# Edge convolution on one core: one-hot row picks in float32r instead of bf16, and a second picked tile in two chunks of five

## What is computed

```python
h = relu(layernorm(x))                                   # no scale, no shift
feat = concat([h[dst], h[src] - h[dst]], axis=-1)
m = relu(feat @ W1 + b1) @ W2 + b2                       # one row per edge
out = x + where(isneginf(segment_max(m, dst)), 0, segment_max(m, dst))
```

## Time and profile before

| what | value |
|---|---|
| median of 3 runs | 3946.11 us (3945.49 to 3949.43) |
| profiled execution, first to last instruction (span) | 3943.7 us |
| what lies around the span (median less span; no separate time of the profiled execution is recorded) | 2.4 us |
| setup, until the first chunk is turned | 488.7 us |
| 313 chunks, until the last store of states | 3798.5 us |
| last part (carry between lanes, gather of maxima, output) | 145.2 us |

### The profile page before, as it was taken

One profiled execution on the slowest core, in us unless ns is written; L12 is line 12 of the kernel. 1 busy time (PEld: TensorE's weight loads), 2 busy tenths in 40 slices (PEclk: granted clock), 3 DMA queues, 4 the chain that ended last, 5 costly groups with the idle time before them and its releaser, 6 DMA issues.

```text
span 3943.7 us, 67318 instructions
## 1 busy us (share of the span) xinstructions
PE 3133.0 (79%) x16627; PEld 1717.1 (44%) x16627; DVE 2582.5 (65%) x7825; ACT 955.1 (24%) x3840; POOL 2963.9 (75%) x3103
## 2 busy tenths in 40 slices
PE   3100099999999999999988889898898898888820
PEld 2000055555555555555544444444444454444410
DVE  5210088788777777787777777777677777767731
ACT  4420022222222222222222222222222222222200
POOL 6777777777777777777777777777777777777766
PEclk8555599999999999999999999999999999999965
DMA  9994133333333333333333333333333333333332
GB/s 372 376 415 192 36 93 95 95 95 94 95 92 91 94 95 95 93 94 91 91 88 85 88 89 87 85 88 87 85 88 88 85 88 88 85 87 87 84 91 49
DMA packets 226373, 443.25 MB, mean 112 GB/s; under 512 B 76740, under 2 KB 81721, under 8 KB 215363
## 3 DMA queue, kind: packets, MB, share of 16 engines
q1 hardware_dynamic: 77508, 220.45, 17.0%
q0 software_dynamic: 100496, 106.38, 13.0%
q10 hardware_dynamic: 47977, 112.13, 7.6%
HBM read 220.98 MB, written 217.71 MB: 111 GB/s over the span
## 4 chain that ended last, share of the span: by engine, by line
POOL 42%; issue 19%; SPq 19%; DMA 9%; PE 9%; DVE 1%; ACT 0%; POOLq 0%; ACTq 0%; DVEq 0%
POOL rows L440 38%; SPq L375 10%; DMA a_edges<-rows 8%; PE ps_g L739 8%; SPq L373 5%; POOL a_rows L496 2%; POOL a_edges L463 2%; SPq L374 2%; PE ps_m L758 1%; SPq L390 1%; DMA row_idx<-in_src_dram 1%; PE ps_t L749 1%; DVE state L983 0%; DVE a_fill L952 0%; DMA a_fill<-a_edges 0%
## 5 line engine op out<-in xcount | busy, mean ns | idle before, releaser
L440 POOL DMA_INDIRECT rows<-b_table,src_idx x2780 | 2657.2, 956 | 847.7 <-issue 844.6
L739 PE MATMUL ps_g<-shared,dst_all 128*128 128x512 bf16 x11433 | 2578.1, 380 | 1.6 <-DVE dst_all L1012 1.4
L739 PEld LDWEIGHTS ps_g<-shared,dst_all 128*128 128x128 bf16 x11433 | 1106.1, 98 | 1222.5 <-issue 12.3
L952 DVE SCALAR_TENSOR_TENSOR a_fill<-a_fill,keep 128x64 f32<-128x64 f32 x3125 | 874.1, 280 | 352.3 <-DMA a_fill<-a_edges 329.4
L983 DVE SCALAR_TENSOR_TENSOR state<-state,keep,ps_m 128x64 f32<-128x64 f32 x3125 | 861.2, 276 | 110.3 <-PE ps_m L758 64.6
L600 ACT ACTIVATE dst_all<-ident_h,key_octet 128x128 f16<-128x128 f16 x309 | 123.6, 400 | 2233.3 <-DVE state L983 2232.6
L969 DVE TENSOR_TENSOR rows<-rows,a_fill 128x512 f32<-128x512 f32 x625 | 279.5, 488 | 521.2 <-DMA rows<-b_table,src_idx 520.9
L758 PE MATMUL ps_m<-w_diag,zt 128*128 128x128 f32 x3126 | 426.7, 284 | 225.0 <-ACT zt L622 220.7
L610 ACT ACTIVATE dst_all<-ps_g,dst_all 128x64 f32<-128x64 f32 x2472 | 539.2, 343 | 0.0
L758 PEld LDWEIGHTS ps_m<-w_diag,zt 128*128 128x128 f32 x3126 | 384.3, 193 | 342.8 <-ACT zt L622 326.3
L749 PE MATMUL ps_t<-ident,rows 128*128 128x128 f32 x1563 | 224.0, 274 | 224.9 <-DVE rows L969 224.9
(11 more groups left out here) (122 smaller groups left out, 441.3 us busy)
## 6 DMA issues: line engine op xcount, KB each, us to landing
a_edges<-rows SPq DMA_DIRECT2D x80, 1250.0 KB, 14.9
a_fill<-a_edges SPq DMA_DIRECT2D x312, 320.0 KB
states<-state ACTq DMA_DIRECT2D x312, 320.0 KB
rows<-b_table SPq DMA_DIRECT2D x4608, 0.2 KB
rows<-b_table,src_idx POOLq DMA_INDIRECT x2780, 2.5
a_fill<-b_table ACTq DMA_DIRECT2D x12, 256.0 KB, 8.8
shared<-in_x_dram SPq DMA_DIRECT2D x5, 560.0 KB
b_table<-shared ACTq DMA_DIRECT2D x5, 560.0 KB
```

The lines of the kernel that those rows point to most:

```text
L440: nc.gpsimd.indirect_dma_start(out=rows[:, c % RING, t * C:(t + 1) * C], out_offset=None, in_=b_table, in_offset=at(src_idx[:, q % SRC_RIN ...
L739: last = nc.tensor.matmul(ps_g[:, half, :], key_is[:, half, g, :], table[:, g, t, :], start=(g, t) == (0, 0), stop=g == PAGES - 1)
L952: nc.vector.scalar_tensor_tensor(here, before, flag(c, 0, t), here, ALU.mult, ALU.add).then_inc(fill_step, 1)
```

## The change

The table holds two parts per value in place of three: the float with its lower 12 mantissa bits cleared, and the rest. Both are stored as float32r, and the one-hot matrices too, so a pick is 12 x 2 + 1 = 25 matmuls. The chunks c from 3 on with c % 5 in (1, 3) have two picked tiles, and POOL gathers one tile less there. Three key matrices (`KEY_RING`) are held in place of two, and two of `masked`; `ps_g` keeps two banks. Key matrices and `masked` move to the memory of `blocks` and `dst_all`. The last tiles of a chunk are the picked ones, and SP's tile is the one ahead of them.

```diff
-    PARTS = 3
+    PARTS = 2
+    TOP_BITS = -(1 << 12)
+    PICKS_MOST = 2
     def picks_in(c):
-        return FIRST_PICK <= c < CHUNKS
+        if not FIRST_PICK <= c < CHUNKS:
+            return 0
+        return 2 if c % 5 in (1, 3) else 1
+    def picks_of(c):
+        return [(picks_below(c) + i, i) for i in range(picks_in(c))]
+    KEY_RING = 3
...
-        return CHUNK - 1 - helped(c) if picks_in(c) else CHUNK
+        return CHUNK - picks_in(c) - helped(c)
...
+        table = nc.alloc_sbuf_tensor_at("table", [P, PAGES, PARTS, OCTET * C], F32R, offset=shared_at)
...
+        key_is = [nc.alloc_sbuf_tensor_at(f"key_is{s}", [P, PAGES, P], F32R, offset=at_byte)
+                  for s, at_byte in enumerate((blocks_at, blocks_at + PAGES * P * 4, dst_all_at))]
...
             def mask(c):
-                n = pick_number(c)
-                act.wait_ge(picked, n + 1 + FREE)
-                act.wait_ge(octets_marked, c // BATCHED + 1)
-                act.wait_ge(chosen, n + FREE)
-                for o in range(OCTET):
...
+                for n, i in picks_of(c):
+                    act.wait_ge(picked, n + 1 + FREE)
+                    act.wait_ge(octets_marked, c // BATCHED + 1)
+                    act.wait_ge(chosen, n - 1 + FREE)
+                    for o in range(OCTET):
...
-                for t in range(PARTS):
-                    if t >= 1:
-                        act.wait_ge(page_left, 1 + g * (PARTS - 1) + t)
-                    nc.scalar.activation(table[:, g, t, :], page[:, g % 2, :], ACT.Copy).then_inc(page_part, 1)
+                act.wait_ge(page_cut, g + 1)
+                nc.scalar.activation(table[:, g, 0, :], page_top[:, :].bitcast(F32), ACT.Copy).then_inc(page_part, 1)
...
-            def pick(c, pages):
-                n = pick_number(c)
+            def pick(n, pages):
                 half = n % 2
                 if pages[0] == 0:
                     pe.wait_ge(keys_matched, n + 1 + FREE)
                     pe.wait_ge(octet_masked, n - 1 + FREE)
                 for g in pages:
                     for t in range(PARTS if g < PAGES - 1 else 1):
-                        last = nc.tensor.matmul(ps_g[:, half, :], key_is[:, half, g, :], table[:, g, t, :],
+                        last = nc.tensor.matmul(ps_g[:, half, :], key_is[n % KEY_RING][:, g, :], table[:, g, t, :],
...
-                if picks_in(c + PICK_AHEAD):
-                    pick(c + PICK_AHEAD, range(PAGES_FIRST))
+                for n, i in picks_of(c + PICK_AHEAD)[:1]:
+                    pick(n, range(PAGES_FIRST))
                 for g, n in groups(tiles):
...
-                if picks_in(c + KEYS_AHEAD):
-                    turn_keys(c + KEYS_AHEAD)
-                if picks_in(c + PICK_AHEAD):
-                    pick(c + PICK_AHEAD, range(PAGES_FIRST, PAGES))
+                turn_keys(c + KEYS_AHEAD)
+                for n, i in picks_of(c + PICK_AHEAD):
+                    pick(n, range(PAGES_FIRST if i == 0 else 0, PAGES))
...
+                nc.vector.tensor_scalar(page_top[:, :], page[:, g % 2, :].bitcast(I32), TOP_BITS, None,
+                                        ALU.bitwise_and).then_inc(page_cut, 1)
+                dve.wait_ge(page_cut, g + 1)
+                nc.vector.tensor_tensor(table[:, g, 1, :], page[:, g % 2, :], page_top[:, :].bitcast(F32),
+                                        ALU.subtract).then_inc(page_left, 1)
...
                     if picks_in(c):
-                        dve.wait_ge(chosen, pick_number(c) + 1 + FREE)
+                        dve.wait_ge(chosen, picks_below(c + 1) + FREE)
...
             def match_keys(c):
-                dve.wait_ge(keys_turned, n + 1 + FREE)
-                dve.wait_ge(picked, n - 1 + FREE)
...
+                for n, i in picks_of(c):
+                    dve.wait_ge(keys_turned, n + 1 + FREE)
+                    dve.wait_ge(picked, max(n - KEY_RING + 1, 0) + FREE)
...
-                    if t == CHUNK - 2 and picks_in(c + CHOOSE_AHEAD):
-                        choose(c + CHOOSE_AHEAD)
+                    for n, i in picks_of(c + CHOOSE_AHEAD):
+                        if t == CHUNK - 2 + i * LEAD:
+                            choose(c + CHOOSE_AHEAD, n, i)
```

More of the change, by code:

```diff
@@ L6 @@
 F32 = mybir.dt.float32
+F32R = mybir.dt.float32r
 BF16 = mybir.dt.bfloat16
@@ L65, in edge_conv, with picked_tile, helped_tile @@
     FIRST_PICK = PICK_AHEAD
+    PICKS_MOST = 2
     def picks_in(c):
-        return FIRST_PICK <= c < CHUNKS
-    def pick_number(c):
-        return c - FIRST_PICK
+        if not FIRST_PICK <= c < CHUNKS:
+            return 0
+        return 2 if c % 5 in (1, 3) else 1
     def picks_below(c):
-        return max(0, min(c, CHUNKS) - FIRST_PICK)
+        return sum(picks_in(d) for d in range(c))
+    def picks_of(c):
+        return [(picks_below(c) + i, i) for i in range(picks_in(c))]
+    def picked_tile(i):
+        return CHUNK - 1 - i
+    def helped_tile(c):
+        return CHUNK - 1 - picks_in(c)
+    KEY_RING = 3
     HELP_EVERY, HELP_SEMS = 8, 8
@@ L193, in edge_conv @@
         octets = sb("octets", [P, OCTET])
[L194 to L199, removed]
+        key_bits = sb("key_bits", [P, 2, BATCHED, PICKS_MOST], I32)
+        key_octet = sb("key_octet", [P, 2, 2, BATCHED, PICKS_MOST])
+        key_is = [nc.alloc_sbuf_tensor_at(f"key_is{s}", [P, PAGES, P], F32R, offset=at_byte)
+                  for s, at_byte in enumerate((blocks_at, blocks_at + PAGES * P * 4, dst_all_at))]
+        behind = dst_all[:, PAGES * P:]
         key_diag = behind[:, 0:P].bitcast(FP16).rearrange("p (s e) -> p s e", s=2)
[L201 to L204, removed]
+        masked = blocks[:, :, :].rearrange("p s k -> p (s k)")[:, 2 * PAGES * P:2 * PAGES * P + 2 * OCTET * C].bitcast(
+            F32).rearrange("p (s o c) -> p s o c", s=2, c=C)
+        octet_is = behind[:, P:P + MARKS * PICKS_MOST * OCTET].bitcast(F32).rearrange(
+            "p (k i o) -> p k i o", i=PICKS_MOST, o=OCTET)
         ps_t = psum("ps_t", [P, GROUPS, 512])
@@ L285, in edge_conv @@
         page_left = sem("page_left")
+        page_cut = sem("page_cut")
         table_ready = sem("table_ready")
@@ L594, in spread_keys @@
             def spread_keys(c):
-                n = pick_number(c)
                 q, j = divmod(c, BATCHED)
[L598 to L601, removed]
-            def mask(c):
-                n = pick_number(c)
-                act.wait_ge(picked, n + 1 + FREE)
-                act.wait_ge(octets_marked, c // BATCHED + 1)
-                act.wait_ge(chosen, n + FREE)
-                for o in range(OCTET):
-                    last = nc.scalar.activation(masked[:, o, :], ps_g[:, n % 2, o * C:(o + 1) * C], ACT.Copy,
-                                                scale=octet_is[:, c % MARKS, o:o + 1])
-                last.then_inc(octet_masked, 1)
+                for n, i in picks_of(c):
+                    act.wait_ge(keys_split, q + 1)
+                    act.wait_ge(keys_turned, n - 1 + FREE)
+                    nc.scalar.activation(key_diag[:, n % 2, :], ident_h[:, :], ACT.Copy,
+                                         scale=key_octet[:, q % 2, 0, j, i:i + 1]).then_inc(keys_spread, 1)
+            def mask(c):
+                for n, i in picks_of(c):
[3 more added lines that the diff above has]
+                    for o in range(OCTET):
+                        last = nc.scalar.activation(masked[:, n % 2, o, :], ps_g[:, n % 2, o * C:(o + 1) * C], ACT.Copy,
+                                                    scale=octet_is[:, c % MARKS, i, o:o + 1])
+                    last.then_inc(octet_masked, 1)
             def step(c, k, tiles=CHUNK):
@@ L723, in turn_keys @@
             def turn_keys(c):
[L725 to L728, removed]
-            def pick(c, pages):
-                n = pick_number(c)
+                for n, i in picks_of(c):
+                    pe.wait_ge(keys_spread, n + 1 + FREE)
+                    pe.wait_ge(keys_matched, n - 1 + FREE)
+                    nc.tensor.matmul(ps_k[n % 2], ones_h[:, :], key_diag[:, n % 2, :], start=True, stop=True).then_inc(keys_turned, 1)
+            def pick(n, pages):
                 half = n % 2
@@ L919, in _ @@
             for g in range(PAGES):
[L920 to L923, removed]
+                page_loads = g // 2 + 1
+                if g == PAGES - 1:
+                    page_loads += PARTS * (1 + (N % OCTET > 0)) - 1
+                dve.wait_ge(page_loaded[g % 2], 16 * page_loads)
+                if g >= 1:
+                    dve.wait_ge(page_part, g)
+                    dve.wait_ge(page_left, 1 + g)
+                nc.vector.tensor_scalar(page_top[:, :], page[:, g % 2, :].bitcast(I32), TOP_BITS, None,
[3 more added lines that the diff above has]
+                                        ALU.subtract).then_inc(page_left, 1)
             dve.wait_ge(picks_set, 1)
@@ L1018, in choose @@
-            def choose(c):
```

(14 more changed lines are left out.)

47 lines of the change are left out of this document (23 added, 24 removed).

## The result

The changed kernel takes 4449.8 us (median of 4 runs, 4448.0 to 4454.1) against 3945.8 us (median of 4): a ratio of 1.128, 95% interval 1.126 to 1.129. The profiled execution took 4448.0 us, its span is 4446.2. Slower, as forecast, but by 504 us and not by 200, and above the upper end of the range (4215).

What follows compares the result with a forecast made beforehand. Consumers bound through PE's wait for the bank: 56.3 us in five chunks, 11.26 a chunk. Chunk 306's store at 3951, the tail's at 3997, plus 145.2 and 2.4 gave 4145 us; range 3785 to 4215.

Steps and rivals of the forecast that it cites:

- The wait that decides: PE's pick waits at `ps_g`'s two banks for ACT's mask, behind the same step's relu: some 124 times, about 2.4 us each.
- The gain does not arrive: 124 gathers fewer would take 156 us off POOL, but consumers at 11.26 us a chunk bound, so POOL waits for slots.
- SP's 10.02 us: Time a chunk takes at the pace of SP's queue with its row fetches, read from its key loads; unchanged by the change.
- The price of a float32r matmul: PE's picking matmuls of 512 columns: one float32r pass taken as fast as bf16, 0.2157 us, with weight loads hidden.
- The rival of dearer matmuls: PE's picking matmuls cost more: about 4830 us with exposed loads, about 6200 at 0.431 us each; chance 10% together.
- exposed weight loads: PE's float32 weight loads not hidden: 0.11 us more a matmul, 2.2 us a chunk, about 4830 us.
- The faster rival: Mask runs early enough that PE doesn't stand at the bank: 3840 us, or 3790 at SP's and POOL's pace; chance 12%.
- (3798.5 - 156 - 501) / 312: Pace the consumers would have to keep for POOL's whole 156 us gain to arrive, given as 10.08 us a chunk.

Runs made afterwards that it cites:

- run 2: Changed kernel with ACT masking the first pick of a doubled chunk one step earlier, PE's order unchanged: 4017.0 us, ratio 1.018 to the kernel before.
- run 1: Changed kernel with the whole pick behind the product with W2 in steps c = 1 and 4 modulo 5: 3889.5 us, ratio 0.985 to the kernel before.
- run 5: Changed kernel with the early mask and, in steps c = 1 and 4 modulo 5, only three pages (6 matmuls) ahead of the product with W2: 3823.9 us.
- run 6: Changed kernel with nine unused matmuls put into each of two idle times of PE: 4265.6 us, ratio 1.081 to the kernel before.
- run 8: Changed kernel with table and one-hot matrices in bf16, plus nine unused matmuls in each of two idle times of PE: 4153.5 us, ratio 1.053.
- run 3: Changed kernel with table and one-hot matrices in bf16 in place of float32r: 4422.9 us, ratio 1.119 to the kernel before.
- run 7: Changed kernel with 64 weight columns in place of 128 in all picking matmuls but a pick's first and last: 4425.5 us, ratio 1.121.

## Why the prediction was right, and where it was wrong

- **The wait that decides: right.** Its place, its count (123 for 124), its length (2.47 us for 2.45) and what is queued behind it are as foretold; run 2 takes the wait away and all but 71 us of the loss goes; runs 1 and 5 also move matmuls behind the product with W2, and are faster than the kernel before.
- **The gain does not arrive: right.** POOL's 124 gathers went and it waited for ring slots instead. In run 5 the consumers keep a pace near SP's 10.02 us, and 122 of the 156 us come.
- **The price of a float32r matmul: mis-sized.** Taken at bf16's 0.2157 us, measured at 0.230 (mean of the spacings under 0.3 us at the full clock), plus about 0.08 on the first of a batch. The step that failed is the one from the earlier trace rows: they give 0.215 us for a record of 256 float32 columns, and that one pass of 512 columns goes at exactly bf16's pace was inferred from them, not read. It was worth 112 us (runs 6 and 8), where the range allowed 62.
- **A term left out: the clock.** The prediction computed 2.45 us of idle time per stall and then went on at 0.2157 us a matmul. The drops that follow cost 184 us (run 6). The late stretch of the trace of before gave no warning: PE waits there 147 times for relu, at most 2.1 us, and the granted clock is 1.00. But the stage of the earlier trace rows did. The same four records that take 1.13 us there, at the full clock, take 2.07 us five microseconds earlier, behind an idle time, with a granted clock of 0.50:

```profile
56.71 2.07 PE L700 MATMUL ps_m<-w_diag,ht 128*125 128x256 f32 x4 [5.40 <-ACT ht L536]
```

I should have given the stall an upper bound with matmuls at twice the time, 0.43 us. The Trainium skill, TensorE: Matmul & The Clock Gate, "HAM oscillation — how this bites in real kernels", says that idle gaps between bursts of matmuls throttle the clock again. The trace agrees that gaps do it, with 0.54 and 0.59 granted after the two; but the gaps that the page tells of are longer than 2.18 and 2.47 us, and here the measurement decides.

- The two add up: 4145 forecast, 8 us of its own error (4153.5 in run 8), 112 for the stream, 184 for the clock, together 4449. Taken in the other order, the same 296 us are 269 for the clock (runs 3 and 8) and 27 for the stream (run 3 and the changed kernel): the clock is the larger part either way. Each alone would have put the result above the range's 4215 us: run 6 has the dear matmuls without the falls of the clock and takes 4265.6 us, run 3 the falls without the dear matmuls and takes 4422.9.
- The rival of dearer matmuls had its mechanism in part, not its size; exposed weight loads are ruled out by run 7. The faster rival priced the stall's absence alone at 3840 us; run 2, which has just that, took 4017, as its matmuls are dearer too (112 us) and the clock still falls in c = 3. That run 5 lies near 3840 is luck: it also moves eight matmuls.
- One sum of the prediction is slightly off: (3798.5 - 156 - 501) / 312 is 10.07, not 10.08. Nothing rests on it.

A third bank for `ps_g`, the plain way to remove the wait, was not tried; `ps_t`, `ps_m`, `ps_s`, `ps_g` and `ps_x` hold eight such banks already.

## What to carry to other kernels

Before a second item goes into a step, follow each ring (here two banks) to the point in the other engine's order where a slot is freed, and see whether that point waits for the same step. If it does, what stands in the order behind the wait counts too: taking away the wait alone, with the fall of the clock behind it, was worth 433 us; moving the 14 matmuls, and the wait ahead of them, behind the product that others wait for, 560. And price a new idle time of PE twice, once for itself and once, as an upper bound, for the matmuls after it at half the clock. It is a bound only: with float32r, one of two equal waits brought the fall and the other mostly didn't.

## What the runs showed of the hardware that was not expected

- A float32r matmul of 128x512 leaves one record and streams at 0.230 us at the full clock, bf16 at 0.216 (runs 3 and 8); at half the clock the spacing is 0.427, the same as bf16's. The excess shows at the full clock alone, and its cause is open; it doesn't depend on the number of weight columns (run 7).
- Shorter work of PE can go with a slower clock: with bf16 in run 3 the granted clock was 0.92 against 0.95, and 27 us came of a gain that is 112 with the idle times filled. Matmuls whose result nobody reads made the kernel 184 us faster (run 6).
